# Attention with all four key tiles' products with V in one slot, x's columns a slot sooner, and three probability buffers in strict rotation

## The reference

```python
x = _ln(src) * (1.0 + scale) + shift
q = (x @ Wq + bq).reshape(B, S, N_HEAD, HEAD_DIM).transpose(0, 2, 1, 3)   # k, v alike
scores = einsum('bhqd,bhkd->bhqk', q / sqrt(HEAD_DIM), k) + attention_bias
probs = softmax(where(src_mask, -inf, scores), axis=-1)
ctx = einsum('bhqk,bhkd->bhqd', probs, v)
x = x + (ctx @ Wo + bo)
ff = _gelu2((_ln(x) * g2 + beta2) @ W1 + b1) @ W2 + b2      # x + ff, then the rotation
```

## Time and profile before

| | us |
|---|---|
| median of three runs | 3349.51 (3343.0 to 3351.04) |
| the profiled execution | 3342.54 |
| its span, first to last instruction | 3340.7 |
| PE busy | 3179.0 (95% of the span) |
| POOL busy | 2011.5 (60%) |
| DVE busy | 2134.5 (64%) |
| ACT busy | 1852.4 (55%) |
| DMA, mean over the span | 235 GB/s |

### The profile page before, as it was taken

One profiled execution on the slowest core, in us unless ns is written; L12 is line 12 of the kernel. 1 busy time (PEld: TensorE's weight loads), 2 busy tenths in 40 slices (PEclk: granted clock), 3 DMA queues, 4 the chain that ended last, 5 costly groups with the idle time before them and its releaser, 6 DMA issues. The chain is left out here.

```text
span 3340.7 us, 52375 instructions
## 1 busy us (share of the span) xinstructions
PE 3179.0 (95%) x16592; PEld 2383.4 (71%) x16592; DVE 2134.5 (64%) x4445; ACT 1852.4 (55%) x4041; POOL 2011.5 (60%) x1247
## 2 busy tenths in 40 slices
PE   5999999999999999999968999999999999999998
PEld 4677777677677767767637678687777867777787
DVE  3777777777777777777757654544555555454542
ACT  2777777777777777777725343332434434243343
POOL 3888888888878888878745634434333343433413
PEclk9999999999999999999989999999999999999999
DMA  5988899888899888898857567575766757676565
GB/s 188 265 262 264 251 276 270 258 262 260 257 272 267 264 255 262 261 266 258 252 150 259 205 219 238 173 253 178 255 208 203 245 182 249 193 246 214 189 203 169
DMA packets 440433, 785.15 MB, mean 235 GB/s; under 512 B 57025, under 2 KB 106177, under 8 KB 440161
## 3 DMA queue, kind: packets, MB, share of 16 engines
q1 hardware_dynamic: 440160, 781.82, 76.0%
HBM read 591.76 MB, written 89.19 MB: 204 GB/s over the span
## 5 line engine op out<-in xcount | busy, mean ns | idle before, releaser
L676 POOL TENSOR_TENSOR biasm<-biasm,maskb 128x1024 f32<-128x1024 f32 x512 | 1091.2, 2147 | 243.7 <-DMA biasm<-in_fside_Bx16xSxS_dram 241.8
L1395 PE MATMUL ps_out<-w_ring,g_hi 128*128 128x512 f32 x2048 | 678.3, 398 | 21.7 <-issue 19.4
L1375 PE MATMUL ps_first<-h_hi,w_ring 128*128 128x512 f32 x1792 | 557.8, 393 | 20.4 <-DVE tmp L1842 10.8
L1613 POOL TENSOR_TENSOR g_lo<-g_now,g_hi 128x512 fp32r<-128x512 f32 x128 | 168.4, 1316 | 626.9 <-ACT g_hi L1492 626.9
L781 PE MATMUL ps_score<-k_rows,q_rows 96*128 96x512 f32 x1024 | 493.8, 482 | 3.6 <-issue 3.3
L832 ACT ACTIVATE probT<-ps_probT 128x512 f32<-128x512 f32 x512 | 304.4, 595 | 309.6 <-PE ps_probT L794 307.3
L1395 PEld LDWEIGHTS ps_out<-w_ring,g_hi 128*128 128x128 f32 x2048 | 386.8, 189 | 113.3 <-issue 33.1
L921 DVE CUSTOM_DVE_ANT_0 prob_first<-ps_score,biasm 128x512 f32<-128x512 f32 x512 | 346.5, 686 | 181.6 <-PE ps_score L781 144.9
L921 DVE CUSTOM_DVE_ANT_0 prob_last<-ps_score,biasm 128x512 f32<-128x512 f32 x512 | 346.5, 686 | 132.7 <-PE ps_score L781 118.3
L794 PE MATMUL ps_probT<-ident,prob_first 128*128 128x128 f32 x2048 | 395.0, 274 | 14.8 <-DVE probT L501 12.7
L1375 PEld LDWEIGHTS ps_first<-h_hi,w_ring 128*128 128x128 f32 x1792 | 339.3, 190 | 93.9 <-DVE w_ring L1732 12.4
(11 more groups left out here) (159 smaller groups left out, 5610.2 us busy)
## 6 DMA issues: line engine op xcount, KB each, us to landing
biasm<-in_fside_Bx16xSxS_dram SPq DMA_DIRECT2D x512, 512.0 KB, 5.6
w_ring<-w_parts SPq DMA_DIRECT2D x240, 512.0 KB, 3.7
w_ring<-w_parts SPq DMA_DIRECT2D x392, 256.0 KB, 3.4
k_rows<-k_hi SPq DMA_DIRECT2D x512, 64.0 KB, 4.7
q_rows<-q_hi SPq DMA_DIRECT2D x512, 64.0 KB, 3.2
xn<-in_x_dram SPq DMA_DIRECT2D x16, 1024.0 KB, 7.3
normal_rows<-xn SPq DMA_DIRECT2D x16, 1024.0 KB, 8.2
k_rows<-k_lo SPq DMA_DIRECT2D x256, 64.0 KB, 4.3
```

The lines of the kernel that those rows point to most:

```text
L676: pool.tensor_tensor(tile, tile, maskb[:, 2 * half:2 * half + 2, :], ALU.add).then_inc(masked.sem, 1)
L1375: mm = pe.matmul(ps[:, BANK[n], :], w1r[:, place, w, cols], h[:, n, c, :], start=(c == 0 and k == 0 and not onto), stop=(c == 1 and k == 2 ...
L1395: mm = pe.matmul(ps_out[:, t, :], a[:, k % 2, cols], w2r[:, k % VR, w, :], start=(m == 0 and n == 0), stop=(m == NF - 1 and n == 2))
L1613: pool.tensor_tensor(GLO[:, k % 2, :], src, GHI[:, k % 2, :].bitcast(F32), ALU.subtract).then_inc(glo_done.sem, 1)
```

## The change

- The products with V of all four key tiles of a group run in slot 2 of the next group; slot 0 has none. The first of them waits for the last head's four transposed tiles.
- x's columns are completed in slots 30, 32, 33 and 35 in place of 31, 33, 34 and 35, and DVE takes them in slots 31, 33, 34 and 36. On ACT x's high part comes ahead of the exponential of its slot. The last q projection of this batch has its high part in slot 29 and its low part in slot 30, one sooner each; the first k projection's low part moves from slot 9 to 8.
- The buffer of the first two query tiles' probabilities is (16b + j) mod 3, counted through all batches, so that a buffer always comes back after three heads.

```diff
-    buffer_of = [j % 3 for j in range(H - 1)] + [1]
-              (31, 1, [("x", 0)]), (33, 1, [("x", 1)]), (34, 1, [("x", 2)]), (35, 1, [("x", 3)]),
+              (30, 1, [("x", 0)]), (32, 1, [("x", 1)]), (33, 1, [("x", 2)]), (35, 1, [("x", 3)]),
-    HI_AT = {("k", 2): 7, ("q", 2): 9, ("k", 3): 25, ("q", 3): 30, ...
-    OUT_AT = {("x", 0): 32, ("x", 1): 34, ("x", 2): 35, ("x", 3): 36, ("k", 2): 9, ... ("q", 3): 31,
+    HI_AT = {("k", 2): 7, ("q", 2): 9, ("k", 3): 25, ("q", 3): 29, ...
+    OUT_AT = {("x", 0): 31, ("x", 1): 33, ("x", 2): 34, ("x", 3): 36, ("k", 2): 8, ... ("q", 3): 30,
-    def probs(j, i):
-        return prob_first[:, buffer_of[j], i, :] if i < NT // 2 else prob_last[:, j % 2, i - NT // 2, :]
+    def probs(b, j, i):
+        return prob_first[:, (H * b + j) % 3, i, :] if i < NT // 2 else prob_last[:, j % 2, i - NT // 2, :]
     def probs_before(b, j, i):
-        if i >= NT // 2:
-            return (b, j - 2) if j >= 2 else (b - 1, j + H - 2)
-        same = [k for k in range(H) if buffer_of[k] == buffer_of[j]]
-        k = same.index(j)
-        return (b, same[k - 1]) if k > 0 else (b - 1, same[-1])
+        return divmod(H * b + j - (3 if i < NT // 2 else 2), H)
...
-                    for kt in ((i, i + 1) if before is not None and h == 0 and i % 2 == 0 else ()):
+                    for kt in ((0, 1, 2, 3) if before is not None and h == 0 and i == 2 else ()):
...
# ACT, in each slot: the exponential (line 848) now stands behind x's high part (line 859)
```

More of the change, by code:

```diff
@@ L419, in attention_stage @@
     assert len(order) % 2 == 0 and len(qk_order) == 2 * NG
-    HI_AT = {("k", 2): 7, ("q", 2): 9, ("k", 3): 25, ("q", 3): 30, ("k", 4): 39, ("q", 4): 43, ("k", 5): 55, ("q", 5): 59}
-    OUT_AT = {("x", 0): 32, ("x", 1): 34, ("x", 2): 35, ("x", 3): 36, ("k", 2): 9, ("q", 2): 11, ("v", 2): 13, ("v", 3): 16, ("k", 3): 27, ("q", 3): 31,
+    HI_AT = {("k", 2): 7, ("q", 2): 9, ("k", 3): 25, ("q", 3): 29, ("k", 4): 39, ("q", 4): 43, ("k", 5): 55, ("q", 5): 59}
+    OUT_AT = {("x", 0): 31, ("x", 1): 33, ("x", 2): 34, ("x", 3): 36, ("k", 2): 8, ("q", 2): 11, ("v", 2): 13, ("v", 3): 16, ("k", 3): 27, ("q", 3): 30,
               ("k", 4): 41, ("q", 4): 45, ("v", 4): 48, ("k", 5): 57, ("q", 5): 61, ("v", 5): 65}
@@ L794, in body @@
                             mm = pe.transpose(ps_probT[:, k % 2, tq * P:(tq + 1) * P],
-                                              probs(j, tq)[:, i * P:(i + 1) * P], ident[:, :])
+                                              probs(b, j, tq)[:, i * P:(i + 1) * P], ident[:, :])
                         mm.then_inc(turned.sem, 1)
@@ L843, in body @@
                             .then_inc(wide_done.sem, 1)
[L844 to L851, removed]
                     if mode != END:
@@ L861, in body @@
                                 .then_inc(xh_done.sem, 1)
+                    t = score_tile(mode, b, j, i)
+                    if t is not None:
+                        tb, tj, ti = t
+                        maxed.wait(act, tb, NT * tj + ti)
+                        e = act.activation(probs(tb, tj, ti), probs(tb, tj, ti), ACT.Exp,
+                                           bias=negmax[:, tj % 2, ti:ti + 1], scale=-1.0,
+                                           accum_out=sums[:, (tj // GH) % 2, ti, tj % GH:tj % GH + 1])
+                        e.then_inc(exped.sem, 1)
+                    if mode != END:
                         for f in [f for f in order if HI_AT.get(f) == slot and runs(mode, f)]:
@@ L920, in body @@
                         dve.sem_inc(dve_waited, 1)
-                        dve.tensor_tensor_reduce(probs(tj, ti), ps_score[:, (TL * tb + n) % NS, :],
+                        dve.tensor_tensor_reduce(probs(tb, tj, ti), ps_score[:, (TL * tb + n) % NS, :],
                                                  biasm[:, bias_place(tb, n // 2)[0], n % 2, :],
```

## The result

| | before | after |
|---|---|---|
| median | 3343.59 (5 runs) | 3316.62 (3308.66 to 3322.35, 5 runs) |
| ratio, 95% interval | | 0.9907 (0.9886 to 0.9928) |
| profiled execution | 3342.54 | 3308.66 |
| its span | 3340.7 | 3306.2 |
| last score tile of the stage at | 1675.7 | 1649.7 |

Faster by 27 us (31 by the ratio) where 54.7 were forecast. The median before has come down from 3349.51 to 3343.59 with two more executions and now lies beside the profiled one, so the 7.0 us that the forecast adds to reach 3295 was scatter. The stage that was changed gives 26.0 of the 34.5 us by which the profiled span is shorter. The rest, 8.5, lies in the second stage, whose code is the same; over the executions of this study it took 1653 to 1665, so that is scatter. A second measurement of the changed kernel gave 0.9906 (0.9892 to 0.9921); its stage ended at 1652.3.

What follows compares the result with a forecast made beforehand. The prediction took PE to bound the attention stage. 21.1 + 18.5 + 12.3 + 5 + 4.2 − 6.4 = 54.7 us gave a profiled 3287.8, plus 7.0 a median of 3295; own range 3283 to 3307, stated range 3281 to 3322.

Steps and rivals of the forecast that it cites:

- the price of a visit: Products with V: 0.33 us for going in and out, paid once per group in 64 groups, gains 21.1 us.
- Rival 3: Products with V: the 0.33 us is paid per key tile, 21 us fewer gained: 3316; chance 0.06.
- x's columns: Slots 30 to 36: waits of 2.34 us per batch become 1.11, gaining 18.5 us in 15 batches.
- the buffers: Slot 57: with reuse at distance three it takes 1.38 us, not 2.15; 0.77 x 16 = 12.3 us gained.
- k's low part: Slot 8: it lies two slots ahead of slot 10's v units, whose wait goes: 5 us gained.
- Slot 49: Group 3: PE's transposes wait 0.4 us for DVE's copy of slot −1, costing 6.4 us over 16 batches.
- Clock: Behind slot 36: spells at 1.2 GHz in three batches go, gaining 4.2 us; ends 0 and 5.
- rival 2: Slots 30 to 33: spells at 1.2 GHz come in most batches, 21 us, and 4.2 are not won: 3320; chance 0.10.
- Rival 4: Block of products: pv_done seen only when all has drained, 2.9 us per batch, 46 us: 3341; chance 0.06.
- Rival 5: Slots 38 to 52: four bias tiles per batch come 1.1 us late each, 72 us slower: 3367; chance 0.05.
- Transfers: Slots 28 to 54: DMA engines full, but a ring of five covers bias tiles and rows; nothing beyond 0.4 us.
- rival 1: Slots 28 to 54: the full DMA stretch takes back its slots' gain, 24 us: 3319; chance 0.12.

Runs made afterwards that it cites:

- part 3: Changed kernel with later moments of x: 3314.79; plus later load of x: 3318.88; store of x in slot 17: 3327.13; that store plus later moments: 3320.03.
- part 2: Kernel before and changed kernel, each with bias transfers after the first five bringing only one of two tiles: 3335.68 and 3285.99.

## Why the prediction was half right

The measured 3316.6 lies outside the forecast's own range (3283 to 3307), and inside the stated one only because that took in rivals 1 to 3. The time alone cannot part these (3319, 3320, 3316); the traces do.

**Held: the price of a visit.** 0.33 per visit, 3.77 for the block forecast; a block slot takes 3.84 over 0.67, of which 0.09 is PE's transposes starting late behind DVE's copy of slot −1, so 3.75. Rival 3 (0.33 per key tile, over 4.0) is out. The 0.09 was forecast at nothing in groups 0 and 1, and is the one small error there: 2 x 0.09 x 15 = 2.7 us.

**Held: x's columns.** Slot 32's wait 0.54 in the walk, 0.55 measured (1.66 − 1.11, with x1 four transposes); slot 33 0.38 and 0.28 (5.23 − 1.11 − 3.84); slot 36 0.19 and 0.26; slot 35 nothing and nothing. **Held: the buffers**, 0.77. **k's low part**: slot 10 0.29 shorter, 4.4 us for 5. **Slot 49**: 0.50 over 4.51 in batch 4, 0.42 in the mean, forecast 0.4. **Clock**: in slots 28 to 53 the stage before has three spells at the lower clock, all at slot 36; the changed kernel has none there and one in batch 0, at slot 46, so rival 2 is out for it. Slots 30 to 33, with their transposes, brought none, until the early store made PE stand in them (part 3): the rival names a place where spells do come once waits of 0.7 to 0.8 us are added.

**Rival 4** (all key tiles seen at the block's end) is out: DVE's wait for x1's high part, which needs key tile 0 gone, is 1.9 us a batch (26.9 in 14), as the walk has it (from 534.9 to 536.63, 1.7), not 2.7 more. **Rival 5** is out in its form: DVE's waits for POOL grew by 0.5 us in the earlier trace rows's group and fell by 0.8 in the other (10.2 to 9.4). Bias did come late, but it hit PE through x's low parts in POOL's queue, a path that no rival had.

**Failed: "Transfers. ... the bias tiles and rows asked for there are covered by a ring of five, so I cost this at nothing beyond the 0.4 above".** A bias transfer of that stretch takes 9.3 us to land in batch 4, in place of 7.7, and the ring of five did not cover it. (That the shortened work asks a full set of engines for the same transfers sooner is the likely reason; no run shows it by itself.) The waits that come are irregular (batches 1 to 13 take 97.6 to 101.2), at x's low part, at stacked rows, at the moments; with half the bias they all but go (part 2), and they move when one is taken away (part 3). That was rival 1, 24 us for 3319, with a chance of 0.12; measured 3316.6. Its cause was right and its chance too low. Its price was near by luck: the transfers cost some 20 us, spread over more slots than it says and not as a fixed length of the stretch (40.5 to 43.7 us), and 4.3 of the gap come from the last batch, which has another cause. Against it I put that 12% of the stage's DMA time is free and that rows come several us ahead. The first is an average, of which the full stretch got nothing; the second did not hold, ACT waited up to 4.9 us for rows.

The Trainium skill, "DMA: Bandwidth & Descriptors", section "Specifications", gives a core some 358 GB/s of HBM; beside the 289 GB/s moved in that stretch this makes an estimate of 69 GB/s of room. The trace does not agree: at 289 GB/s the share was 1.06, and halving the bias gave the time back, so the measurement decides. (The prediction says of that figure that it would leave "the second rival" worth nothing; it means the first.)

**Failed, smaller: the last batch.** It has no fill units, so ACT's and DVE's standing for the block is uncovered in slots 31 to 33 (+1.1) and 47 to 49 (+0.9): +2.6 in all where −1.69 was forecast. "Nothing is late there" was worked out for batches with fill units only. With half the bias it is still 80.4 against 78.5, so transfers are not its cause; without the merge it is 78.4.

Open: why batches of the same code differ by 3 us in the full stretch, in which the full engines moved 303 GB/s in batch 1 and 283 in batch 10. A sixth bias buffer would tell whether a deeper ring covers it; it was not tried.

## What to carry to other kernels

Read the DMA share in the stretch where a change takes time out, not over the stage: a share at or above 1 there is a warning that transfers may land later when the work gets shorter, and that time saved inside may come back as a wait elsewhere, here in the stretch or just behind it. Read the time from issue to landing beside it. To know what an edit is worth apart from that, halve the transfers in both kernels and compare. Before you read a run that moves a transfer, look where the queue really issues it. And price a change again for the first and last passes of a pipeline, where the work that covers its waits is missing.

## What was not expected

The 16 DMA engines were full at 289 GB/s with a mix of 512 KB bias tiles and 64 KB rows. At a share of 1 that would be 289 / 1.06 = 273 GB/s, by batch 1 303 / 1.05 = 289, and with half the bias 206 / 0.72 = 286. Taking a wait away there gave nothing in three kernels, and moving the store cost 14 us against the changed kernel (3327.13 to 3313.17).
